# Adaptive-norm transformer block on one core: a reordered prologue, weight tests in pairs on ScalarE, gates computed per feature

## The chip, the cores and the metric

The kernel runs on one core of one Trainium2 chip. The core has five engines with instruction queues of their own: TensorE (PE, with its weight load PEld), VectorE (DVE), ScalarE (ACT), GpSimd (POOL) and SyncE (SP), which only issues DMAs here. They wait for one another through semaphores. The metric is the device time of one execution in microseconds (us).

## The reference, cut to what matters

For four sequences (B = 4) of 2048 tokens with 256 features, one block of attention and one feed-forward network:

```python
mod = (_silu(c) @ wmod).reshape(4, 6, 1, 256)
sa, ca, ga, sb, cb, gb = (mod[:, k] for k in range(6))
ga = (2 * (ga >= 0) - 1) * jnp.maximum(jnp.abs(ga), 0.25)      # gb alike
h = _layernorm(x) * (1 + ca) + sa
x = x + ga * attention(h)        # chunks of 64 tokens, a 64x64 state per head carried from chunk to chunk
h = _layernorm(x) * (1 + cb) + sb
x = x + gb * ffn(h)              # silu(x w1 s) * (x w2 s), two 1024x1024 gelu layers, w3
```

The attention needs, for each chunk and head, the inverse of a unit triangular 64x64 matrix whose entries carry powers of a decay per head. The feed-forward weights are ternary (-1, 0, 1) in the inputs drawn here, but the kernel must be right for others too.

## The kernel before, in words

**Steps.** The 2048 tokens are 32 chunks of 64. A step handles one chunk of all four sequences: 128 partitions hold two sequences' 64 tokens each, twice (NB = 2). Step n computes attention of chunk n, layers l1 and l2 of the feed-forward network of chunk n-1, and layers l3 and w3 (`y`) of chunk n-2. Each engine walks the same list of named items (`mixed`, `walk`), and each engine does its part of an item. So an engine's order is the order of the list, written out by hand, and nothing else moves it. Steps 3 to 30 are a loop of 14 steps that runs twice.

**The path chosen at run time.** A feed-forward weight that is exact in its upper 16 bits can be multiplied in a fast form (`w_hi`, rounded to fp32r). At the start all 22 slots of weights (8 blocks of 128x128 each, 512 KB) are loaded into `w_raw`; the lower 16 bits of each are tested (`check`), each slot is cast to `w_hi` (`round`), and one flag from all tests (`any_low`, `row_low`, `flag_i`) decides by a branch on every engine between two whole programs. All the feed-forward work lies behind that branch.

**The prologue.** Ahead of the branch stand: the modulation (TensorE L1220, L1235, L1239), its gates (`gates()` on VectorE, `gates` on the others), the decay powers (written to DRAM at L734, read back shifted into `hank` at L738, turned by TensorE L1246 and L1247 into the tables of `tables()`), the first norm (`pre("norm", 1)`, L767, L771), the whole of step 0 (the list `alone`: attention of chunk 0 with nothing beside it) and the front part of step 1 (the list `opening`). Behind the branch comes the rest of step 1 (the list `second`), then step 2 and the loop.

**Names that the steps below use.** `fs` is the forward substitution in 8x8 blocks: `fs 0` sets it up, `fs 1` to `fs 3` are six dependent turns of a shuffle, a product and a subtraction (L842, L844, L846). `expand`, `n 1` to `n 3`, `mi`, `upd` build the inverse; `new` and `state` make the new values and the state; `attn_out` multiplies by `wr_sb` and adds the residual (`gah`, `base` on GpSimd, `x1` on VectorE). `norm2` and `ln2` are the second norm, `parts` splits its result (`xh`, `xl`). `square_t` (L666) is ScalarE's copy between `n 2` and `n 3`. `rounded` counts casts; TensorE waits for it before l1 (L1006), before each l2 item and before step 2's transposes (L1091).

In the kernel before, the tests are divided between ScalarE (13 slots, L644) and VectorE (9 slots, L797), one slot at a time, all 22 casts are GpSimd's (L569), and the gates are computed on 4 partitions x 512 features and spread by a matmul with a selector (L1080).

## Time and profile before

| | |
|---|---|
| median of 3 runs | 1912.02 us (1909.98 to 1915.57) |
| the profiled execution, its own time | 1917.14 us |
| its span in the profile | 1915.3 us |
| TensorE busy | 1824.8 us, 95% |
| VectorE, ScalarE, GpSimd busy | 62%, 50%, 33% |
| granted TensorE clock, mean | 0.978 |

The span is what lies between the first and the last record of the profile; the profiled execution's own time is 1.8 us longer. Of the 40 equal slices of the profile's second part (47.9 us each), TensorE is busy 40, 40 and 70% in the first three and 90% or more in all others, and its granted clock is 0.7, 0.5 and 0.8 of full speed in the first three (its two levels are 1.2 and 2.4 GHz) and full in all others. The DMA engines are 80% busy in the first slice and under 10% after it.

### The profile page before, as it was taken

Reading aid. Unit: us, or ns where it says so; the run is one execution under the profiler, and the core shown is the slowest. Engines: PE = TensorE matmul, PEld = TensorE weight load, DVE = VectorE, ACT = ScalarE, POOL = GpSimd, SP = SyncE. Lnnn points to the kernel's source line nnn. Section 1 sums busy time; section 2 is a strip of 40 time slices with the busy share of each in tenths; the row PEclk is TensorE's granted clock in tenths of the full one; section 3 lists DMA queues with packets and bytes.
Section 4 is the critical chain, followed back from the end, with each engine's and each line's share of the span. In section 5 each row is a group of like instructions: output and inputs, shape, how many; then the busy total and the mean of one; then the engine's idle time right before and its main releaser. Section 6 shows DMA issues by size and latency. Waiting matters only on the chain.

```text
span 1915.3 us, 66858 instructions
## 1 busy us (share of the span) xinstructions
PE 1824.8 (95%) x28586; PEld 1746.7 (91%) x28586; DVE 1181.6 (62%) x3051; ACT 965.4 (50%) x2304; POOL 632.1 (33%) x708
## 2 busy tenths in 40 slices
PE   4479999999999999999999999999999999999999
PEld 2369999999999999999999999999999999999998
DVE  4766665666666666666566666566666656666632
ACT  2235454555555555545455545455555545554554
POOL 3434333223323323333332333332333332333211
PEclk7589999999999999999999999999999999999999
DMA  8000000000000000000000000000000000000000
GB/s 301 24 3 19 19 13 19 8 19 19 18 16 17 19 8 19 19 19 13 19 12 16 18 19 13 19 16 11 19 19 19 13 19 8 19 19 19 9 7 12
DMA packets 32721, 43.75 MB, mean 23 GB/s; under 512 B 8156, under 2 KB 24680, under 8 KB 32424
## 3 DMA queue, kind: packets, MB, share of 16 engines
q1 hardware_dynamic: 30736, 37.19, 6.5%
q8 instruction: 228, 3.74, 0.8%
q10 hardware_dynamic: 1688, 2.26, 0.4%
q14 instruction: 69, 0.57, 0.1%
HBM read 22.52 MB, written 8.39 MB: 16 GB/s over the span
## 4 chain that ended last, share of the span: by engine, by line
PE 59%; issue 19%; POOL 10%; DVE 9%; ACT 2%; DMA 1%; SPq 0%; POOLq 0%; DVEq 0%; ACTq 0%
PE mlp L1006 38%; PE mlp L1065 6%; PE solo L1006 4%; PE solo L1105 3%; POOL rinv L537 2%; POOL rg L577 2%; PE solo L1127 2%; POOL gah L550 2%; POOL base L554 2%; DVE h L767 1%; DVE h L771 1%; POOL rstd L537 1%; PE duo L1147 1%; PE duo L1151 1%; DVE kg L815 1%
## 5 line engine op out<-in xcount | busy, mean ns | idle before, releaser
L1006 PE MATMUL mlp<-act_hi,w_hi 128*128 128x256 f32 x4096 | 1007.6, 288 | 2.9 <-DVE full L903 2.1
L1006 PE MATMUL mlp<-act_lo,w_hi 128*128 128x256 f32 x4096 | 972.3, 279 | 0.0
L1006 PEld LDWEIGHTS mlp<-act_hi,w_hi 128*128 128x128 f32 x4096 | 770.4, 188 | 15.0 <-DVE full L903 2.6
L1006 PEld LDWEIGHTS mlp<-act_lo,w_hi 128*128 128x128 f32 x4096 | 771.1, 188 | 1.6
L718 ACT ACTIVATE full<-mlp,scale_sb 128x256 f32<-128x256 f32 x512 | 244.2, 477 | 562.0 <-PE mlp L1006 561.6
L790 DVE TENSOR_TENSOR act_lo<-full,act_hi 128x256 fp32r<-128x256 f32 x512 | 250.0, 488 | 404.0 <-ACT act_hi L719 404.0
L591 POOL TENSOR_TENSOR act_lo<-full,act_hi 128x256 fp32r<-128x256 f32 x256 | 186.5, 735 | 518.4 <-ACT act_hi L708 518.4
L719 ACT ACTIVATE act_hi<-mlp,scale_sb 128x256 fp32r<-128x256 f32 x512 | 240.6, 470 | 0.0
L557 POOL TENSOR_TENSOR lv<-gram,level_mask 128x256 f32<-128x256 f32 x192 | 159.8, 859 | 110.6 <-DVE low L831 104.9
L1006 PE MATMUL mlp<-xh,w_hi 128*128 128x256 f32 x768 | 187.7, 283 | 7.1 <-issue 5.5
L1006 PE MATMUL mlp<-xl,w_hi 128*128 128x256 f32 x768 | 187.0, 282 | 0.0
L537 POOL TENSOR_TENSOR rstd<-ve,minus_half 128x2 f32<-128x2 f32 x64 | 49.3, 770 | 391.5 <-DVE ve L757 391.5
L1006 PEld LDWEIGHTS mlp<-xh,w_hi 128*128 128x128 f32 x768 | 145.7, 190 | 7.7 <-issue 5.9
L903 DVE SCALAR_TENSOR_TENSOR full<-mlp,scale_sb,gate 128x256 f32<-128x256 f32 x192 | 92.7, 483 | 96.1 <-ACT gate L703 96.1
L703 ACT ACTIVATE gate<-mlp,scale_sb 128x256 f32<-128x256 f32 x192 | 91.3, 475 | 117.7 <-PE mlp L1006 117.7
L1006 PEld LDWEIGHTS mlp<-xl,w_hi 128*128 128x128 f32 x768 | 146.1, 190 | 0.0
L1065 PE MATMUL mlp<-w_hi,act_hi 128*128 128x256 f32 x512 | 123.3, 284 | 0.0
L1065 PE MATMUL mlp<-w_hi,act_lo 128*128 128x256 f32 x512 | 122.2, 280 | 0.0
L537 POOL TENSOR_TENSOR rinv<-ssm,minus_half 128x8 f32<-128x8 f32 x32 | 52.6, 1645 | 207.3 <-DVE ssm L780 207.3
L708 ACT CAST act_hi<-full 128x256 fp32r<-128x256 f32 x256 | 101.7, 397 | 12.3 <-DVE full L903 12.3
L1065 PEld LDWEIGHTS mlp<-w_hi,act_hi 128*128 128x128 f32 x512 | 96.5, 188 | 0.4
L1065 PEld LDWEIGHTS mlp<-w_hi,act_lo 128*128 128x128 f32 x512 | 96.6, 189 | 0.0
(157 smaller groups left out, 2642.0 us busy)
## 6 DMA issues: line engine op xcount, KB each, us to landing
w_raw<-in_wts SPq DMA_DIRECT2D x22, 512.0 KB, 13.6
xin<-in_x SPq DMA_DIRECT2D x64, 128.0 KB, 2.8
out_y<-y SPq DMA_DIRECT2D x64, 128.0 KB, 2.5
kg<-r SPq DMA_DIRECT2D x64, 126.0 KB
wmod_sb<-in_wmod ACTq DMA_DIRECT2D x1, 1024.0 KB, 8.6
kg<-last SPq DMA_DIRECT2D x64, 2.0 KB
last<-r SPq DMA_DIRECT2D x64, 2.0 KB, 1.7
wmod_sb<-in_wmod ACTq DMA_DIRECT2D x1, 512.0 KB, 5.3
```

Of the source, the lines that this page charges most:

```text
L537: pool.tensor_tensor(dst[:], src[:], minus_half[:, 0:src.shape[1]], ALU.pow).then_inc(done, 1)
L557: return pool.tensor_tensor(lv[slot][:, e].rearrange("p (b q) n -> p b (q n)", b=NB), gram[:, e].rearrange("p (b q) n -> p b (q n)", b=NB) ...
L591: pool.tensor_tensor(act_lo[0][:, k, :], full[k % 3][:], act_hi[0][:, k, :].bitcast(F32), ALU.subtract).then_inc(l_ready[0], 1)
L703: act.activation(gate[k % 2][:], gated[k % 3][:, 0:TOK], ACT.Silu, scale=scale_sb[:, 0, k:k + 1]).then_inc(l_act[0], 1)
L708: act.copy(act_hi[0][:, j, :], full[j % 3][:]).then_inc(l1_hi, 1)
L718: act.activation(full[k % 2][:], mlp[k % 2][:, 0:TOK], ACT.Gelu, scale=s)
L719: act.activation(act_hi[layer % 2][:, k, :], mlp[k % 2][:, 0:TOK], ACT.Gelu, scale=s).then_inc(l_act[layer], 1)
L790: dve.tensor_tensor(act_lo[layer % 2][:, k, :], full[k % 2][:], act_hi[layer % 2][:, k, :].bitcast(F32), ALU.subtract).then_inc(l_ready[la ...
L903: dve.scalar_tensor_tensor(full[k % 3][:], up, s, gate[k % 2][:], ALU.mult, ALU.mult).then_inc(prod_ready, 1)
L1006: mm = pe.matmul(dst, *general_ops, start=is_first and i == 0, stop=is_last and i == 1)
L1065: mm = pe.matmul(mlp[k][:, 0:D], *ops, start=j == 0 and i == 0, stop=j == HK - 1 and i == 1)
L1105: mm = pe.matmul(solo[0][:, b * D:(b + 1) * D], hT[:, kt, b, :], wv_sb[:, kt, :], start=kt == 0, stop=kt == KT - 1)
```

## The change

Six things are changed, all ahead of step 2; the items of the loop are the same in the same order.

1. The tests are ScalarE's alone, two slots at a time (11 tests of 2048 halves in place of 22 of 1024), and VectorE has none. ScalarE also does 17 of the 22 casts: 4 in step 0, 5 at the end of `opening`, 8 behind the items of l2. GpSimd does the last 5.
2. The gates are computed as columns: TensorE makes them as 128 features x 4 sequences (L1223 of the kernel after), VectorE works on 128x16 and 128x8 elements instead of 4x512, ScalarE spreads them over 64 columns each (`spread`), and TensorE transposes them (8 transposes) into the rows where the selector's product stood. One small input is gone (`sel`).
3. On ScalarE the two copies of the second half of the modulation (`mods`) stand ahead of the wait for the decay powers and the read of `hank`; on SyncE the weight loads from the fifth on wait until `hank` is there.
4. On TensorE the two matmuls with `hank` stand behind the transposes of the first norm (item `tables`) in place of ahead of step 0.
5. `alone` and `opening` are reordered: in `alone`, `fs` is no longer interrupted, the residual (`residual`) and the product with alpha (`wr`) come later; in `opening`, `gram` stands ahead of the second norm on TensorE, and `intra`, `fs 0` and five casts stand ahead of the branch.
6. In `second`, VectorE does `u` and all of `fs 1` to `fs 3` before the first l1 item; `expand`, `far` and `n 1` to `n 3` stand between the l1 items, and `keys` to `attn_out` between the l2 items as in a step of the loop.

```diff
-CHECKS_ACT = {0: (0, 1, 2), 2: (4, 6, 7, 9), 4: (11, 13), 7: (15, 17, 19, 20)}
-CHECKS_DVE = {1: (3, 5), 3: (8,), 4: (10,), 5: (12,), 6: (14, 16), 7: (18, 21)}
+CHECKS = {0: (0,), 1: (1, 2, 3, 4, 5), 2: (6,), 3: (7, 8, 9, 10)}
+ROUNDS_ACT = {0: range(0, 4), 1: range(4, 9)} | {2 + k: (9 + k,) for k in range(8)}
+ROUNDS_POOL = {2 + k: (17 + k,) for k in range(5)}
...
-    alone = [("check", 0), ("ready", 0), ("start", 0), ("tables", 0), ("gram", 0), ("pred", 0), ("values", 0), ("check", 1), ("intra", 0), ("fs", 0), ("far", 0),
-             ("check", 2), ("round", 0), ("fs", 1), ("gates", 0), ("fs", 2), ("fs", 3), ("expand", 0), ("n", 1), ("check", 3), ("round", 1), ("n", 2),
-             ("check", 4), ("n", 3), ("check", 5), ("keys", 0), ("mi", 0), ("check", 6), ("upd", 0), ("round", 2), ("new", 0), ("check", 7), ("state", 0),
-             ("attn_out", 0)]
+    alone = [("check", 0), ("ready", 0), ("start", 0), ("spread", 0), ("tables", 0), ("gram", 0), ("pred", 0), ("values", 0), ("gates", 0), ("intra", 0),
+             ("u", 0), ("fs", 0), ("fs", 1), ("fs", 2), ("fs", 3), ("expand", 0), ("far", 0), ("check", 1), ("round", 0), ("residual", 0), ("n", 1), ("n", 2),
+             ("check", 2), ("wr", 0), ("n", 3), ("keys", 0), ("mi", 0), ("upd", 0), ("new", 0), ("check", 3), ("state", 0), ("attn_out", 0)]
...
-    opening = [("start", 0), ("norm2", 0), ("ln2", 0), ("ln2", 1), ("gram", 0), ("pred", 0), ("values", 0), ("parts", 0), ("silu", 0)]
+    opening = [("start", 0), ("gram", 0), ("norm2", 0), ("ln2", 0), ("ln2", 1), ("pred", 0), ("values", 0), ("intra", 0), ("fs", 0), ("parts", 0),
+               ("round", 1), ("silu", 0)]
+    second = [("u", 0), ("fs", 1), ("fs", 2), ("fs", 3)]
     for item in layers[:len(layers) - len(late)]:
-        second += [item] + ([("round", 3 + item[1])] if item[0] == "l2" else []) + after_layer.get(item, [])
+        second += [item] + {("l1", 0): [("expand", 0), ("far", 0)], ("l1", 1): [], ("l1", 2): [("n", 1)]}.get(item, between.get(item, []))
+        second += [("round", 2 + item[1])] if item[0] == "l2" else []
...
             for u in range(SLOTS):
+                if u == 4:
+                    sp.wait_ge(pow_in, 32)
                 sp.dma_start(w_raw[:, SLOT * u:SLOT * (u + 1), :].rearrange("p b n -> p (b n)"), wts[u]).then_inc(hi_in[u // UNIT_SLOTS], 16)
...
+                        for i in CHECKS[k]:
+                            act.wait_ge(hi_in[i], 16 * UNIT_SLOTS)
+                            after(act, checked, i)
+                            words = w_raw[:, UNIT_SLOTS * SLOT * i:UNIT_SLOTS * SLOT * (i + 1), :].rearrange("p b n -> p (b n)")
+                            act.activation(low_bits[:], low_halves(words), ACT.Copy, accum_out=slot_low[:, i:i + 1]).then_inc(checked, 1)
+                    if name == "round":
+                        for u in ROUNDS_ACT[k]:
+                            slot = slice(SLOT * u, SLOT * (u + 1))
+                            act.wait_ge(checked, u // UNIT_SLOTS + 1)
+                            act.copy(w_hi[:, slot, :], w_raw[:, slot, :]).then_inc(rounded[0], 1)
...
                         if isinstance(n, int) and n == 2:
-                            pe.wait_ge(rounded, SLOTS)
+                            pe.wait_ge(rounded[0], 17)
+                            pe.wait_ge(rounded[1], SLOTS - 17)
```

**ScalarE at the start.** The rows are ScalarE's instructions in their order, each with its line, what it writes and reads, its shape and the semaphores it waits for; `decay_powers` and `hank` are the decay powers' way through DRAM, `low_bits` is a weight test. Before:

```order
L734 DMA decay_powers<-pow_row_sb 4x128 [waits pow_row]
L738 DMA hank<-decay_powers 64x4x64 [waits pow_out]
L738 DMA hank<-decay_powers 64x4x64
L740 COPY mods<-duo 128x256 [waits mod_full]
L741 ACTIVATE mods<-duo 128x256
L644 ACTIVATE low_bits,slot_low<-w_raw 128x1024 [waits hi_in0]
```

ScalarE at the same place in the kernel after:

```order
L717 DMA decay_powers<-pow_row_sb 4x128 [waits pow_row]
L719 COPY mods<-duo 128x256 [waits mod_full]
L720 ACTIVATE mods<-duo 128x256
L724 DMA hank<-decay_powers 64x4x64 [waits pow_out]
L724 DMA hank<-decay_powers 64x4x64
L619 ACTIVATE low_bits,slot_low<-w_raw 128x2048 [waits hi_in0]
```

The two copies have moved ahead of the wait for `pow_out`, and one test of two slots follows where three of one slot each did.

**ScalarE in the middle of step 0**, kernel after; `mods<-mlp` are the gates, `w_hi` is a cast of one slot, `square_t` what `n 3` waits for:

```order
L632 COPY mods<-mlp 128x512 [waits gates_spread] x2
L619 ACTIVATE low_bits,slot_low<-w_raw 128x2048 [waits hi_in1,checked,small_in,cols_ready]
L619 ACTIVATE low_bits,slot_low<-w_raw 128x2048 [waits checked,hi_in2]
L619 ACTIVATE low_bits,slot_low<-w_raw 128x2048 [waits checked,hi_in3]
L619 ACTIVATE low_bits,slot_low<-w_raw 128x2048 [waits checked,hi_in4]
L619 ACTIVATE low_bits,slot_low<-w_raw 128x2048 [waits checked,hi_in5]
L624 CAST w_hi<-w_raw 128x1024 [waits checked] x4
L650 COPY square_t<-duo 128x256 [waits square_full]
```

In the kernel before, four tests of one slot stand ahead of the gates' copies and nothing between these and `square_t`; now five double tests and four casts stand there.

**VectorE behind the branch.** The rows are VectorE's from the first of step 1's second part on; `full` is the product of an l1 item, `sub` and `sub_term` are the substitution. Before:

```order
L903 SCALAR_TENSOR_TENSOR full<-mlp,scale_sb,gate 128x256
L822 TENSOR_TENSOR intra<-duo,intra_mask 128x256 x2
L827 TENSOR_TENSOR v<-v,duo 128x2x4x64
L903 SCALAR_TENSOR_TENSOR full<-mlp,scale_sb,gate 128x256
L831 TENSOR_REDUCE low<-lv 128x64
```

VectorE at the same place in the kernel after (the three rows of `sub_row`, `sub_term` and `sub` stand six times before the row of `full`; the first turn is shown, then the last row of the sixth):

```order
L807 TENSOR_TENSOR v<-v,duo 128x2x4x64
L822 STREAM_SHUFFLE sub_row<-sub 128x64
L824 TENSOR_TENSOR sub_term<-sub_row,low 128x64
L826 TENSOR_TENSOR sub<-sub,sub_term 128x64
...
L826 TENSOR_TENSOR sub<-sub,sub_term 128x64
L883 SCALAR_TENSOR_TENSOR full<-mlp,scale_sb,gate 128x256
L829 TENSOR_TENSOR inv<-sub,con 128x256
```

The first product of l1 stood first on VectorE; now it stands behind nineteen instructions of the attention.

## Rows read from the trace of the kernel before

**Rows 1.** By stretch: us; busy PE, PEld, DVE, ACT, POOL (instructions); clock; DMA share; GB/s.
```profile
45.00:75.00 30.00, 10.17 (x416) 9.30 (x416) 25.99 (x53) 12.21 (x24) 17.40 (x17) 0.50 0.07 20
...
180.00:240.00 60.00, 58.90 (x916) 56.74 (x915) 36.70 (x97) 31.08 (x75) 19.86 (x23) 1.00 0.06 16
```

**Rows 2.** The chain of waits, start: start us, us, what.
```profile
11.93 4.77 DMA decay_powers<-pow_row_sb
...
17.39 9.79 DMA hank<-decay_powers
```

**Rows 3.** Timeline of the first norm: start, length, engine, line, work, [idle before <-releaser].
```profile
18.76 0.88 DVE L767 SCALAR_TENSOR_TENSOR h<-xin,mv,mods 128x256 f32<-128x256 f32 x2 [6.20 <-ACT mods L741]
...
22.29 1.64 POOL L537 TENSOR_TENSOR rinv<-ssm,minus_half 128x8 f32<-128x8 f32 x1 [9.06 <-DVE ssm L780]
...
25.99 0.67 DVE L783 TENSOR_TENSOR r<-h,rinv 128x512 f32<-128x512 f32 x1
```

**Rows 4.** DMA issues: KB each, median us from issue to landing.
```profile
xin<-in_x SPq DMA_DIRECT2D x64, 128.0 KB, 2.8
```

**Rows 5.** Timeline, from the tables to the corrected values.
```profile
34.90 1.18 POOL L577 TENSOR_TENSOR rg<-rT,head_decay 128x512 f32<-128x512 f32 x1 [10.97 <-DVE head_decay L936]
...
42.46 0.69 DVE L827 TENSOR_TENSOR v<-v,duo 128x512 f32<-128x512 f32 x1 [4.54 <-ACT v L656]
```

**Rows 6.** Timeline of the substitution, with GpSimd at work and without.
```profile
45.57 3.99 POOL L569 CAST w_hi<-w_raw 128x1024 fp32r<-128x1024 f32 x4
...
46.72 0.95 DVE L846 TENSOR_TENSOR sub<-sub,sub_term 128x64 f32<-128x64 f32 x1
...
52.71 0.23 DVE L846 TENSOR_TENSOR sub<-sub,sub_term 128x64 f32<-128x64 f32 x1
```

**Rows 7.** ScalarE's tests and casts, all of each line: ns min/median/max.
```profile
L644 ACT ACTIVATE low_bits<-w_raw x13: 1056/1057/1060, 18.6 to 74.3; 128x1024 f32<-128x1024 uint16 x13
...
L708 ACT CAST act_hi<-full x256: 393/396/408, 107.1 to 1877.0; 128x256 fp32r<-128x256 f32 x128
```

**Rows 8.** Timeline, step 0 from the third product of the inverse on.
```profile
62.23 1.07 PE L1151 MATMUL duo<-first_two,square_t 32*32 32x32 f32 x64 [1.46 <-DVE first_two L861]
...
70.07 0.59 ACT L686 COPY vn<-solo 128x512 f32<-128x512 f32 x1 [2.11 <-PE solo L1185]
...
76.09 0.68 DVE L871 TENSOR_TENSOR oT<-o_state,duo 128x512 f32<-128x512 f32 x1
```

**Rows 9.** Timeline, second norm, flag and the first layer's start.
```profile
86.52 2.27 DVE L889 SCALAR_TENSOR_TENSOR xn<-x,mv,rstd 128x256 f32<-128x256 f32 x2
...
97.81 0.14 DVE L988 TENSOR_SCALAR flag_i<-row_low 1x1 int32<-1x1 f32 x1
...
102.94 0.55 PE L1006 MATMUL mlp<-xh,w_hi 128*128 128x256 f32 x1 [5.48 <-issue]
```

**Rows 10.** Two stretches of step 1 behind the branch (columns as in rows 1).
```profile
103.00:106.00 3.00, 3.00 (x14) 3.00 (x15) 0.46 (x2) 0.47 (x1) 0.00 (x0) 0.50 0.02 5
...
124.00:127.00 3.00, 3.00 (x30) 2.78 (x33) 0.32 (x1) 0.04 (x1) 0.00 (x0) 0.51 0.02 5
```

**Rows 11.** Timeline of TensorE, step 2's start, and a full step.
```profile
147.61 0.66 PE L1091 MATMUL duo<-con,h 128*128 128x128 f32 x4 [0.99 <-POOL w_hi L569]
...
176.55 0.28 PE L1006 MATMUL mlp<-xh,w_hi 128*128 128x256 f32 x1
...
204.62 0.60 PE L1091 MATMUL duo<-con,h 128*128 128x128 f32 x4
```

**Rows 12.** Chain of waits, one piece per step; then the idle time before L1156.
```profile
385.86 7.54 PE mlp L1006 x64
...
443.30 7.54 PE mlp L1006 x64
...
499.69 7.54 PE mlp L1006 x64
...
  issue: 6.6, 8
```

160 lines of the change are left out of this document (64 added, 96 removed).

## The prediction

> **What bounds the kernel now.** I read the busy times by stretch first. In a stretch of the loop TensorE is busy 58.9 of 60 us at full clock; between 45 and 75 us it is busy 10.2 of 30 us at half clock while VectorE is busy 26.0 [rows 1]. So the loop is TensorE's, and the change leaves the loop's items as they are; what it can win or lose lies ahead of step 2, whose transposes begin at 147.61 us [rows 11]. That moment is what I forecast; the rest is carried along. Then I read the chain of waits at the start and followed it in the timeline: the decay powers' write and their read into `hank`, the tables, the substitution on VectorE, the products of the inverse, VectorE's late `oT`, the second norm, and 5 us between the flag and the first l1 matmul [rows 2, 3, 5, 6, 8, 9].
>
> **First norm and tables.** `h` begins at 18.76 and had waited 6.20 us for ScalarE's copies, which stood behind the wait for the powers' write (landed at 11.93 + 4.77 = 16.70) [rows 2, 3]. With the copies first, `h` begins some 5.1 us earlier, at 13.6. From `h` to `rinv` it is 22.29 - 18.76 = 3.5 us, `rinv` takes 1.64, so `r` can begin at 18.9 in place of 25.99 [rows 3]; the gates, which filled VectorE until then, are now 128x16 elements and end by about 18.8 (seven operations at most 0.23 us each, the price of a 128x64 one [rows 6], from 17.2 on). `hank`: its read took 9.79 us from 17.39, with the weights streaming in the same DMA engines [rows 2]. Now only four slots are ahead. The bounds are 9.79 (no change) and the 2.8 us of an x load twice its size [rows 4]; I take 2.8, since that load runs on a quiet machine as this one then would: 20.2. The transposes of `r` end at 20.7 (0.9 to 1.1 us of TensorE), so `hank` is no longer last. Before, `rg` began 34.90 - 27.18 = 7.7 us behind the landing [rows 2, 5]; of that, 2.6 were the first norm's transposes and `rT`, which now come ahead. So 20.7 + 5.1 puts `rg` at 25.8: **9.1 us ahead**. The weights from the fifth on start at 20.2; 9.4 MB at the 0.4 MB/us that the engines carried before puts the last at about 45, and ScalarE tests them from 60 on: no cost.
>
> By the Trainium skill, "DMA: Bandwidth & Descriptors", Anatomy of one DMA, a DMA has a fixed part of about 2.0 us and the rest goes by bytes. That speaks for the low bound; this trace's 9.79 us differs, and the measurement decides for a loaded machine. By the page `hank` would be there at 19.4 and the sum would not change.
>
> **Substitution.** Up to `u` nothing else changes: 42.46 - 34.90 = 7.6 us [rows 5], so `u` begins at 33.3 and ends at 34.0; `fs 0` ends at 36.0. Of the six turns, two took 4.5 us beside GpSimd's casts (a 128x64 subtraction 0.95 us beside them, 0.23 alone [rows 6]) and four took 3.4 alone. GpSimd now has no casts there, but `far` and the residual, 3 us of it: I take two slow turns and four quick ones, 7.4 us, to 43.4. The product with alpha (2.7 us, in the middle before) is moved behind. So `first_two` is ready at 48.9 on VectorE.
>
> **ScalarE's queue.** The gates' copies end at 35.7 (the eight transposes are 2.1 us at half clock). Then five double tests and four casts stand ahead of `square_t`. A test of 1024 is 1.06 us [rows 7] with 0.19 to read its sum: a double one 2.3 from the rate, 2.5 at most. A cast of 1024 has no row on ScalarE: bounds are the test's 1.06 (same elements, rows 7) and four times the 256-wide cast, 4 x 0.396 = 1.58 [rows 7]; I take 1.06, because the test is the same size. 35.7 + 5 x 2.3 + 4 x 1.06 + 0.4 = 51.9. So `n 3` begins at 52.0, three us later than VectorE would allow, and 62.23 before [rows 8]: **10.2 ahead**. To `vn` it is 7.84 us of unchanged work [rows 8]: 59.9. The state's products end 2.2 us later, and `oT`, which had stood behind four tests on VectorE until 76.09 [rows 8], begins at 62.8: **13.3 ahead**. ScalarE's last four tests end near 70, when `hT` is wanted only at 79.
>
> **Second norm, flag, branch.** From `oT` to `xn` it was 86.52 - 76.09 = 10.4 us [rows 8, 9]; 2.0 of them `xn` stood behind `r` and `rT` on VectorE, though its own inputs were there, and these now come ahead of it. So `xn` begins at 71.2: **15.3 ahead**. From `xn` to the flag the order on TensorE is the same work; `intra` and `fs 0` on VectorE fit under ScalarE's 2.5 us of `h2`. The flag is at 82.5 in place of 97.81, and the 5.0 us of the branch stay: first l1 matmul at 87.6 in place of 102.94 [rows 9], **15.3 ahead**. ScalarE meanwhile does five casts (5.3 us), to 88; if its own branch then takes as long as TensorE's, its first gate is at 93.
>
> **Behind the branch.** VectorE does `u` and six turns, 0.7 + 6 x 0.85 = 5.8 us, before the first product of l1: 93.5. TensorE has three banks, stops after three l1 items, gets `n 1` at 95.1 and l1's fourth item at 96.1. In step 2 the same item began at 176.55 and the next step's transposes at 204.62 [rows 11]: 28.1 us at full clock, to 124.2. To that come: 1.7 us, as after the branch TensorE first runs 3.4 us at half clock (clock 0.50 at 103 to 106 [rows 10]); 2.2 us, as the transposes wait for ScalarE's 17th cast behind the last gelu (0.2 + 0.85 + 1.06), where 0.99 was waited before [rows 11]; 0.6 for `far` beside l1; 1.0 for some six new hand-overs at 0.15 us. 124.2 + 1.7 + 2.2 + 0.6 + 1.0 = 129.7 against 147.61: **17.9 us ahead**. For the profiled execution that is 1917.14 - 17.9 = 1899.2; it stood 5.1 above the median, so for the runs 1912.02 - 17.9 = 1894.1. I forecast 1894.
>
> **The rivals.** *Hank is no quicker* (its read is 9.79 us by its 256-byte pieces and not by the weights). For: the write before it, only 2 KB, also took 4.77 [rows 2]. Against: an x load of twice the bytes takes 2.8 [rows 4]. Tables 6.5 us later, all behind them too, less what ScalarE's queue absorbs (its tests need weights that then come 7 us later too, so nothing): gain 11.6, 1900. Chance 0.10.
>
> *ScalarE is full.* Casts 1.58 and tests 2.5: `n 3` 1.0 + 2.1 later; in l2 a turn of ScalarE is 0.85 + 1.58 = 2.43 against TensorE's 1.88, eight of them with its other 3.2 us make 22.7 against some 20, and the last cast 0.5: 6.3 us in all, gain 12, 1900. For: the 0.396 row. Against: the test's row. Chance 0.11.
>
> *The stalls go further than I count*: the branch on ScalarE is hidden, the three us at `square_t` and the l1 stop come out shorter: gain 23 to 26, 1887. Chance 0.09.
>
> *The loop shifts.* Between 443.30 and 499.69 a step takes 56.39 us, from 385.86 to 443.30 it takes 57.44; the slow ones hold idle time before L1156 with no releaser, 6.6 us in 8 places [rows 12]. If that hangs on where a step's instructions lie, the shorter prologue may move it: 10 more slow steps take 10 us back (1904), all 20 others take 20 (1914). Chance 0.12: 0.05 for at most 10, 0.07 for more.
>
> *The slower one: the clock stays low.* TensorE fell to 0.51 at 124 to 127, after stops of 2 us behind VectorE [rows 10]. If ScalarE's casts between the gelus stop it briefly in each l2 item, all of step 1 from 96 on runs at half clock: the 28.1 us hold some 27 of matmul, which double: 27 - 18 = 9 us slower, 1921. It decides from about 18 us more at half clock on. Against: once VectorE is not late, TensorE has no stops in such items (58.9 of 60 us busy [rows 1]), and ScalarE's turn with a cast, 0.85 + 1.06 = 1.9, is no longer than TensorE's. The Trainium skill, "TensorE: Matmul & The Clock Gate", What's actually happening, says that throttled is the default and activity releases it; the rows agree (0.50 and 0.51 after stops, 1.00 in the loop [rows 1, 10]), and by it a TensorE that is fed from 96 on is soon at full clock. Chance 0.06. My own sum has 0.52 (1889 to 1899).
>
> **Numbers.** Faster by over 0.3% (under 1906.3; 0.3% is what a measurement here tells from none): 0.52 + 0.10 + 0.11 + 0.09 + 0.05 of the loop case = 0.87. Within: 0.07. Slower: 0.06. The range takes in the further gain and both 1900 cases and the smaller loop shift: 1885 to 1906.
>
> **What would show it.** `h` at 13.6, tables at 25.7, `square_t` waiting on ScalarE's queue and not on TensorE, `n 3` at 52, the flag near 82.5, first l1 near 87.6, VectorE's first product near 93.5, step 2's transposes near 129.7 with a wait for ScalarE's cast, and later steps at 56.4 or 57.4. A `hank` landing past 21, a cast over 1.2 us, or a clock of 0.5 past 100 us would make it wrong.

## The result, and the profile after

The changed kernel takes **1883.53 us** (median of 4 runs, 1882.46 to 1885.55), beside 1913.8 for the kernel before on the same chip; the ratio is 0.985, with a 95% interval of 0.982 to 0.987. Five more runs gave 1883.18 and 0.984 (0.983 to 0.985). The prediction had the direction and was too small: 17.9 us forecast, 30 us measured, and 1883.5 lies below the range's 1885.

The profiled execution went from 1917.14 to 1885.55 us, 31.6 less. The same cut that the prediction made, at the transposes of step 2, divides it:

| us | before | after | gain | forecast |
|---|---|---|---|---|
| span up to step 2's transposes | 147.61 | 125.07 | 22.5 | 17.9 |
| span behind them | 1767.7 | 1758.6 | 9.1 | 0 |

So 4.6 us of what was missed lie ahead of step 2, and 9.1 in and behind the loop, whose instructions the change does not touch. The medians put the miss at 10.6 us (1883.5 against 1894.1); the profiled execution of the kernel before was 3 to 5 us above that kernel's medians.

First the stretches (columns as in [rows 1]), to be read beside [rows 1, 10]:

```profile
45.00:75.00 30.00, 17.69 (x450) 14.94 (x439) 16.61 (x37) 18.51 (x29) 8.93 (x9) 0.56 0.10 26
86.00:89.00 3.00, 2.84 (x13) 2.88 (x14) 1.52 (x8) 1.04 (x3) 0.00 (x0) 0.50 0.02 5
92.00:95.00 3.00, 3.00 (x142) 2.84 (x141) 1.90 (x5) 1.83 (x5) 2.60 (x5) 1.00 0.02 5
98.00:101.00 3.00, 3.00 (x18) 3.00 (x16) 0.97 (x2) 1.53 (x4) 0.92 (x2) 0.55 0.00 0
180.00:240.00 60.00, 59.01 (x919) 56.90 (x918) 38.14 (x103) 30.88 (x74) 19.82 (x23) 1.00 0.06 15
```

VectorE's 26 busy us of [rows 1] are 16.6, TensorE's 10.2 are 17.7. Behind the branch the clock is full already at 92, and then falls once more, to 0.55 at 98 to 101.

The timeline of the kernel after, with the lines that answer to [rows 3, 5, 8, 9, 11] (start, length, engine, line, work, idle time before it):

```profile
14.07 0.88 DVE L750 SCALAR_TENSOR_TENSOR h<-xin,mv,mods 128x256 f32<-128x256 f32 x2 [1.54 <-ACT mods L720]
...
19.33 0.69 DVE L766 TENSOR_TENSOR r<-h,rinv 128x512 f32<-128x512 f32 x1 [0.49 <-POOL rinv L512]
...
20.98 1.06 PE L1069 MATMUL solo<-hank,con 128*128 128x256 f32 x2
...
25.98 1.18 POOL L552 TENSOR_TENSOR rg<-rT,head_decay 128x512 f32<-128x512 f32 x1 [6.75 <-DVE head_decay L916]
...
33.42 0.69 DVE L807 TENSOR_TENSOR v<-v,duo 128x512 f32<-128x512 f32 x1 [6.78 <-ACT v L640]
...
44.54 3.87 ACT L624 CAST w_hi<-w_raw 128x1024 fp32r<-128x1024 f32 x4
...
48.31 0.36 ACT L650 COPY square_t<-duo 128x256 f32<-128x256 f32 x1
...
50.64 1.07 PE L1139 MATMUL duo<-first_two,square_t 32*32 32x32 f32 x64 [0.60 <-DVE first_two L841]
...
61.24 0.69 DVE L851 TENSOR_TENSOR oT<-o_state,duo 128x512 f32<-128x512 f32 x1 [2.74 <-PE duo L1183]
...
69.44 2.89 DVE L869 SCALAR_TENSOR_TENSOR xn<-x,mv,rstd 128x256 f32<-128x256 f32 x2
...
81.58 0.14 DVE L967 TENSOR_SCALAR flag_i<-row_low 1x1 int32<-1x1 f32 x1
...
81.77 0.69 DVE L807 TENSOR_TENSOR v<-v,duo 128x512 f32<-128x512 f32 x1
...
86.16 0.55 PE L985 MATMUL mlp<-xh,w_hi 128*128 128x256 f32 x1 [4.93 <-ACT w_hi L624]
...
88.75 0.48 DVE L883 SCALAR_TENSOR_TENSOR full<-mlp,scale_sb,gate 128x256 f32<-128x256 f32 x1 [1.23 <-ACT gate L687]
...
96.46 0.24 PE L1144 MATMUL duo<-inv,step_nt 32*32 32x32 f32 x2 [1.38 <-issue]
...
125.07 0.66 PE L1079 MATMUL duo<-con,h 128*128 128x128 f32 x4 [1.86 <-ACT w_hi L624]
```

Read it from the top. `h`, `r`, the tables' matmuls (right behind the transposes of `r`, not waiting for `hank`) and `rg` stand where the forecast put them, to half a us. From `square_t` on, everything up to the first l1 matmul is one to three us earlier than forecast. The two lines at 81.58 and 81.77 are the surprise: VectorE goes on 0.05 us behind the flag, and its six turns end at 87.5, under TensorE's 4.9 us of waiting; the first product of l1 comes at 88.75, not at 93.5. The row at 96.46 is a stop of TensorE for which the profile names no releaser, in the middle of 64 equal matmuls.

The tests and casts, all of each line (answering to [rows 7]; ns min/median/max):

```profile
L619 ACT ACTIVATE low_bits<-w_raw x11: 1907/1910/1933, 17.9 to 65.2; 128x2048 f32<-128x2048 uint16 x11
...
L624 ACT CAST w_hi<-w_raw x17: 1027/1044/1082, 44.5 to 124.0; 128x1024 fp32r<-128x1024 f32 x17
```

In the loop one piece of the chain of waits, and the same piece one step later (L985 is L1006 of [rows 12]):

```profile
415.61 7.47 PE mlp L985 x64
...
471.71 7.47 PE mlp L985 x64
```

This step takes 56.10 us; the one shown before took 56.39. From transposes to transposes, steps 2 to 30, the middle step takes 56.23 us and took 56.40, which makes 5 us in 29 steps. The other 4 us are long steps: before, nine were over 56.8 us and all steps together stood 8.4 us above 29 middle ones; after, it is four steps and 4.1 us.

### The profile page after: what moved, and what is told of

It is laid out like the page before. It is cut to its first block, busy times and chain, and to the rows that moved or that the text cites. A ratio compares the mean times of both kernels' runs of the same rounds, so it can differ in the third digit from the quotient of the medians.

```text
span 1883.7 us, 66867 instructions
## 1 busy us (share of the span) xinstructions
PE 1821.0 (97%) x28598; PEld 1747.3 (93%) x28598; DVE 1148.9 (61%) x3042; ACT 987.5 (52%) x2318; POOL 613.2 (33%) x691
## 4 chain that ended last, share of the span: by engine, by line
PE 57%; issue 21%; POOL 11%; DVE 8%; ACT 2%; ACTq 0%; POOLq 0%; DVEq 0%
PE mlp L985 36%; PE mlp L1044 6%; PE solo L985 4%; PE solo L1093 3%; POOL rinv L512 3%; POOL rg L552 2%; POOL gah L525 2%; PE solo L1115 2%; POOL base L529 2%; DVE h L754 1%; DVE h L750 1%; POOL rstd L512 1%; DVE ss L761 1%; PE duo L1139 1%; PE duo L1135 1%
## 5 line engine op out<-in xcount | busy, mean ns | idle before, releaser
L985 PE MATMUL mlp<-act_hi,w_hi 128*128 128x256 f32 x4096 | 1009.2, 289 | 0.4 <-POOL act_lo L566 0.2
L985 PE MATMUL mlp<-act_lo,w_hi 128*128 128x256 f32 x4096 | 974.2, 279 | 0.0
L985 PEld LDWEIGHTS mlp<-act_hi,w_hi 128*128 128x128 f32 x4096 | 769.5, 188 | 12.0 <-POOL act_lo L566 0.4
L985 PEld LDWEIGHTS mlp<-act_lo,w_hi 128*128 128x128 f32 x4096 | 771.7, 188 | 1.6
L773 DVE TENSOR_TENSOR act_lo<-full,act_hi 128x256 fp32r<-128x256 f32 x512 | 244.2, 477 | 410.6 <-ACT act_hi L703 410.6
L985 PE MATMUL mlp<-xh,w_hi 128*128 128x256 f32 x768 | 183.1, 280 | 4.9 <-ACT w_hi L624 4.9
L985 PE MATMUL mlp<-xl,w_hi 128*128 128x256 f32 x768 | 182.6, 280 | 0.2 <-issue 0.2
L985 PEld LDWEIGHTS mlp<-xh,w_hi 128*128 128x128 f32 x768 | 146.4, 191 | 5.3 <-ACT w_hi L624 5.3
L687 ACT ACTIVATE gate<-mlp,scale_sb 128x256 f32<-128x256 f32 x192 | 91.0, 474 | 112.1 <-PE mlp L985 96.1
L985 PEld LDWEIGHTS mlp<-xl,w_hi 128*128 128x128 f32 x768 | 146.5, 191 | 0.4 <-issue 0.4
```

The costliest lines, as they stand in the source:

```text
L687: act.activation(gate[k % 2][:], gated[k % 3][:, 0:TOK], ACT.Silu, scale=scale_sb[:, 0, k:k + 1]).then_inc(l_act[0], 1)
L773: dve.tensor_tensor(act_lo[layer % 2][:, k, :], full[k % 2][:], act_hi[layer % 2][:, k, :].bitcast(F32), ALU.subtract).then_inc(l_ready[la ...
L985: mm = pe.matmul(dst, *general_ops, start=is_first and i == 0, stop=is_last and i == 1)
```

## The experiments

In one table, from the profiled execution of each kernel: when step 2's transposes begin, and what is left of the span behind them; then the median of its runs, and the ratio to the kernel before, run beside it. That kernel's own median lay between 1912.1 and 1913.8 from one set of runs to the next, so differences of one or two us between rows are not told from none. Three of the kernels (dve_branch, no_branch, second_old) ran on another chip than the rest. Nor do the profiled executions start alike: `h` begins between 13.1 and 15.0 us in the kernels whose order up to there is that of the kernel after.

| kernel | step 2 at | the rest | median | ratio to before |
|---|---|---|---|---|
| before | 147.61 | 1767.7 | 1913 | 1 |
| after | 125.07 | 1758.6 | 1883.5 | 0.985 (0.982, 0.987) |
| after_again | 124.98 | 1757.4 | 1883.2 | 0.984 (0.983, 0.985) |
| after_pad32 | 126.52 | 1766.1 | 1892.7 | 0.988 (0.985, 0.990) |
| before_shift32 | 146.26 | 1756.8 | 1904.0 | 0.995 (0.994, 0.996) |
| after_align64 | 123.40 | 1766.5 | 1892.9 | 0.989 (0.988, 0.991) |
| act64 | 123.35 | 1748.2 | 1875.1 | 0.981 (0.979, 0.982) |
| dve_branch | 126.22 | 1755.4 | 1881.5 | 0.983 (0.981, 0.985) |
| no_branch | 122.82 | 1757.1 | 1881.8 | 0.984 (0.982, 0.986) |
| second_old | 129.06 | 1760.1 | 1892.1 | 0.990 (0.987, 0.992) |
| no_hold | 133.64 | 1755.1 | 1889.6 | 0.988 (0.986, 0.989) |
| mods_late | 129.66 | 1759.3 | 1889.9 | 0.987 (0.984, 0.989) |
| single_tests | 121.77 | 1757.6 | 1882.4 | 0.984 (0.982, 0.986) |
| pass28 | 122.40 | 1752.6 | 1877.2 | 0.982 (0.980, 0.983) |
| ishift128 | 122.40 | 1755.6 | 1879.9 | 0.982 (0.981, 0.984) |
| best | 122.19 | 1742.9 | 1865.5 | 0.975 (0.973, 0.977) |

### The nine us in the loop: addresses

The change makes `slot_low` 11 numbers long in place of 22. That takes 64 bytes of each partition in place of 96, so all that is allocated later, `xh` and `xl` among it, lies 32 bytes lower.

**after_pad32** (after, with the old addresses)
```diff
     slot_low = sb("slot_low", [SLOTS // UNIT_SLOTS])
+    pad = sb("pad", [8])
```


> The kernel after with an unused tensor of 8 floats behind slot_low, so that every tensor allocated later stands at the address it has in the kernel before (xh and xl 32 bytes past a multiple of 64 in place of on one). Theory A (the address of xh and xl sets the spacing of the l1 matmuls): a normal step goes from 56.17 back to 56.39 us, about 29 times 0.2, so 1889 to 1890 us, with nothing changed ahead of step 2. Rival (the shorter prologue or the queues' order did it, addresses do nothing): 1883 to 1885 us, steps 56.17.

**before_shift32** (before, with the new addresses)
```diff
-    slot_low = sb("slot_low", [SLOTS])
+    pad = sb("pad", [SLOTS // 2])
...
+        slot_low = sb("slot_low", [SLOTS], F32, early)
```


> The kernel before, with slot_low moved into the region that is used again later and an unused tensor of 11 floats in its place, so that all later tensors stand at the addresses of the kernel after, 32 bytes lower. Theory A (address): a normal step 56.39 to 56.17 us, 5 to 6 us off the total, 0.997 of before (1906 to 1908 us), step 2 still begins near 147.6. Rival (address does nothing): ratio 1.000.

**after_again** is the control.


> The kernel after, unchanged, as the control of this call and for a second trace. Both theories: 1883 to 1885 us. If the long steps of the loop (about 1 us longer, idle TensorE ahead of the bursts of 32x32 matmuls) belong to places in the program, they are the same steps as in the first trace (steps 4 and 18 to 20 of the marks); if they are chance, they are others.

Both point to the address, and more strongly than expected. 32 bytes up cost the kernel after 9.5 us, 32 bytes down give the kernel before 9.4. Their "rest" columns simply trade places: 1766.1 and 1756.8 against 1757.4 to 1758.6 and 1767.7. One run of after_pad32 fell out: of its five, four took 1891.6 to 1894.5 us and one 1882.6; it has no trace, and I can't explain it. The groups of l1's matmuls in the loop (205 to 1760 us) show where; the number behind the busy time is the mean ns of one. First before and before_shift32:

```profile
L1006 PE MATMUL mlp<-xh,w_hi 128*128 128x256 f32 x649 | 157.2, 281 | 0.0
```
```profile
L1007 PE MATMUL mlp<-xh,w_hi 128*128 128x256 f32 x672 | 157.3, 277 | 0.0
```

and then after and after_pad32:

```profile
L985 PE MATMUL mlp<-xh,w_hi 128*128 128x256 f32 x672 | 157.5, 277 | 0.0
```
```profile
L986 PE MATMUL mlp<-xh,w_hi 128*128 128x256 f32 x672 | 162.8, 281 | 0.0
```

The 4 ns go with the address, not with the kernel: 64 such matmuls a step make 0.26 us. TensorE's time in the middle one of steps 3 to 29, divided by what it works on (from the start of one matmul to that of the next, us), shows that this is not the only part that goes with the address:

| | l1 | l2 and l3 | w3 | attention |
|---|---|---|---|---|
| before | 8.05 | 31.50 | 3.81 | 13.09 |
| before_shift32 | 7.80 | 31.61 | 3.83 | 12.88 |
| after | 7.80 | 31.63 | 3.83 | 12.88 |
| after_pad32 | 8.05 | 31.56 | 3.81 | 13.05 |

L1 gains 0.25 us from the lower addresses, attention 0.2, and l2 and l3 lose 0.1. Which operand does it in the attention was not tried. The middle step follows: 56.40 and 56.45 at the old addresses, 56.19 to 56.23 at the new ones, 6 or 7 us in 29 steps. Of before_shift32's larger gain behind step 2 (10.9 us in the profiled executions) the rest is again fewer long steps, four against nine. The control's long steps were others than those of the first trace: one over 56.8 us (59.0, step 16), where the first has four (steps 3, 18, 19 and 30). So their number is not a property of the program alone, and whether the address has a hand in it is not shown.

**after_align64** asks whether 64 bytes are the unit.
```diff
+            if -(-int(np.prod(shape)) // 8) % 2:
+                c.enter_context(nc.sbuf_tensor(name + "_pad", [P, 8], F32))
```


> The kernel after with every tensor in SBUF begun on a multiple of 64 bytes (act_hi and act_lo, which in the kernel after are 32 past one, as well as xh and xl). Theory A in its wide form (any moving operand off a multiple of 64 costs): l2 and l3, four times as many matmuls as l1, gain too, up to 0.5 us a step, 1870 to 1878 us. In its narrow form (only some reads are slower when off): 1883 to 1885, since the kernel before with act_hi on a multiple of 64 had no quicker l2. Rival (address does nothing): 1883 to 1885.

They are not: it lost 9.7 us to after_again, and its `xh` matmul takes 283 ns. So I measured the spacing by itself.

**addresses**
```diff
+            for step32 in range(64):
+                off = 8 * step32
+                for w in range(4):
+                    for j in range(KT):
+                        for part in range(2):
+                            at = off + 512 * part + 256 * j
+                            mm = pe.matmul(mlp[w % 2][:, 0:TOK], w_hi[:, KT * w + j, :], data[:, at:at + 256],
+                                           start=j == 0 and part == 0, stop=j == 1 and part == 1)
```


> The kernel after, with 1024 more matmuls of l1's form behind its last output, on TensorE alone: 16 (four weight pairs, two halves each, two operands 2048 bytes apart) at each of 64 start addresses of the moving operand, 32 bytes apart, over 2048 bytes, all at full clock. Nothing else runs then. Theory A1 (TensorE's own reads cost more at some addresses): the spacing of the starts changes with the address, from about 113 to 117 ns, with a period that the row shows. Rival A2 (the address only matters because other engines read or write SBUF at the same time): all 64 are spaced alike, within 1 ns.

Nine of the 64 groups, 16 matmuls each, in TensorE's timeline. They begin 160, 192, 224, 0, 32, 64, 96, 128 and 160 bytes past a multiple of 256:

```profile
1925.57 2.05 PE L1242 MATMUL mlp<-act_hi,w_hi 128*128 128x256 f32 x16
...
1927.46 2.05 PE L1242 MATMUL mlp<-act_hi,w_hi 128*128 128x256 f32 x16
...
1929.35 2.07 PE L1242 MATMUL mlp<-act_hi,w_hi 128*128 128x256 f32 x16
...
1931.25 2.07 PE L1242 MATMUL mlp<-act_hi,w_hi 128*128 128x256 f32 x16
...
1933.15 2.04 PE L1242 MATMUL mlp<-act_hi,w_hi 128*128 128x256 f32 x16
...
1935.03 1.99 PE L1242 MATMUL mlp<-act_hi,w_hi 128*128 128x256 f32 x16
...
1936.86 2.05 PE L1242 MATMUL mlp<-act_hi,w_hi 128*128 128x256 f32 x16
...
1938.75 2.08 PE L1242 MATMUL mlp<-act_hi,w_hi 128*128 128x256 f32 x16
...
1940.66 2.05 PE L1242 MATMUL mlp<-act_hi,w_hi 128*128 128x256 f32 x16
```

From start to start over 16, that is 118.1, 118.1, 118.8, 118.8, 117.5, **114.4**, 118.1, 119.4 ns, and then it repeats. A1 holds, A2 falls: no other engine runs here. Counted like this, with the weights at 128 past, the sizes of the tensors put `xh` and `xl` of the kernel after at 64 past (114.4), of the kernel before at 96 (118.1), of after_align64 at 128 (119.4): the order of 277, 281 and 283. By the sweep, l1 gains 64 x 3.7 ns = 0.24 us a step.

**pairs** moves the weights as well.
```diff
+                                at, wat = 8 * m32 + 512 * part + 256 * j, 8 * w32 + 128 * (KT * w + j)
+                                mm = pe.matmul(mlp[w % 2][:, 0:TOK], weights[:, wat:wat + 128], data[:, at:at + 256],
```


> The kernel after, with 1024 more matmuls of l1's form behind its last output: 8 start addresses of the weights, 32 bytes apart, times 8 of the moving operand, 32 bytes apart, 16 matmuls for each pair. The earlier sweep, with the weights at 128 past a multiple of 256 bytes, gave spacings of 114.7 to 119.6 ns that repeat every 256 bytes of the moving operand's address. Theory D1 (the two reads collide: what counts is the distance between the two addresses modulo 256): each row of eight is the row before shifted by one, and its best is where the moving operand stands 64 below the weights. Rival D2 (the moving operand's own address counts): all eight rows alike, best at 64 past a multiple of 256, 114.7 ns. D3 (chance of the layout): no order.

Weights at 64 past, moving operand at 0 and at 64 past; then weights at 128 past, moving operand at 64 past:

```profile
1961.52 2.00 PE L1242 MATMUL mlp<-act_hi 128*128 128x256 f32 x16
...
1965.12 2.08 PE L1242 MATMUL mlp<-act_hi 128*128 128x256 f32 x16
...
1995.48 1.99 PE L1242 MATMUL mlp<-act_hi 128*128 128x256 f32 x16
```

The same operand at 64 past is among the slowest with weights at 64 and the quickest with weights at 128, where 16 matmuls take 0.09 us less. All 64 spacings, worked out from the records (ns, first start to last of a group, over 15):

```
weights   moving operand at, past a multiple of 256 bytes
at        160   192   224     0    32    64    96   128
160     125.8 118.2 117.9 119.2 119.1 117.3 114.5 117.8
192     118.3 119.5 118.1 117.8 119.3 119.1 117.3 114.5
224     117.8 118.2 119.5 118.2 117.8 119.2 119.1 117.3
  0     117.6 115.5 117.8 119.6 118.1 117.9 119.3 119.1
 32     118.7 117.3 114.7 117.8 119.6 118.1 117.9 119.2
 64     119.6 118.3 117.3 114.7 117.9 119.5 118.2 117.8
 96     117.9 119.9 118.6 118.7 113.6 117.9 119.5 118.1
128     116.7 117.8 119.2 119.1 117.3 114.5 117.8 119.6
```

Apart from a few places, the first above all (125.8), each row is the row above shifted by one. In seven of the eight the best (113.6 to 115.5 ns) stands 64 below the weights; the one exception, weights at 224 with 117.8, I can't explain. D1 holds: the distance modulo 256 counts.

**act64** uses it where it pays most, in l2 and l3.
```diff
+    pad_act = sb("pad_act", [40])
     act_hi = [sb(f"act_hi{i}", [HK, TOK], F32R) for i in range(2)]
...
+    pad_xh = sb("pad_xh", [24])
     xh = sb("xh", [KT, TOK], F32R)
```


> The kernel after with act_hi, act_lo, xh and xl all begun 64 bytes past a multiple of 256 (in the kernel after xh and xl are, act_hi and act_lo are 160 past one), by two unused tensors of 160 and 96 bytes. Theory A1 from the sweep: 118.2 ns becomes 114.7 for the 256 matmuls of l2 and l3 in a step, 0.9 us a step, and 31 steps: 28 us faster than after, 1855, as far as no other engine takes over. Rival (the sweep's numbers do not carry over to the full kernel, where l2's spacing is set by weight loads or other engines): 1883 to 1885. In between, if VectorE or ScalarE set part of a step: 1860 to 1875.

8.1 us faster than after: the direction right, the size a third of the forecast's 28. Most matmuls of l2 and l3 are then 113 to 114 ns apart, but about a third stay at 117 to 119, and before act64 they were on average 117, not the 118.2 of the sweep. L2 and l3 take 31.1 us of a middle step in place of 31.6, where the forecast wanted 0.9 us less, and attention 0.15 more than in the kernel after; the middle step takes 55.9 us in place of 56.2. What keeps the third back was not tried.

### The stop at 95 us, and where instructions lie

**pass28** and **ishift128** ask about TensorE's idle times that nothing releases.
```diff
-PASS = 14
+PASS = 28
```


> The kernel after with the loop's 28 steps in one pass in place of two passes of 14, so that TensorE never jumps back. Theory E (the long steps, 56.9 to 58.7 us near steps 17 to 21, are TensorE's wait for instructions behind the jump back): they vanish, 2 to 3 us faster, 1880 to 1881. Rival (they come from where the instructions lie, or from chance): as many long steps, elsewhere, 1883 +- 1.


```diff
             with pe.If(any_bits > 0):
                 program(True)
+                for _ in range(128):
+                    pe.wait_ge(const_in, 16)
```


> The kernel after with 128 more waits at the end of TensorE's slow path, which is never run; the fast path's instructions then lie that much further on and are otherwise the same. Theory F (TensorE's stalls in the bursts of 32x32 matmuls are waits for instructions, and where the instructions lie decides whether a burst meets one): the stall of 1.4 us at 95 us vanishes or changes by over 0.3 us, long steps are others, total 1879 to 1886. Rival (stalls belong to the work itself, or to the time since the branch): the same 1.4 us at the same matmul, 1883 +- 1.

Neither changes an instruction that is run ahead of the loop, and in both the stop at 95 us is gone. The stretch 95 to 98 us of after (98 to 101 stands above), and both of ishift128:

```profile
95.00:98.00 3.00, 1.62 (x18) 1.50 (x11) 0.42 (x1) 0.00 (x0) 0.46 (x1) 0.88 0.02 5
```
```profile
95.00:98.00 3.00, 2.99 (x76) 2.84 (x63) 1.19 (x3) 1.36 (x5) 1.02 (x2) 1.00 0.02 5
98.00:101.00 3.00, 3.00 (x84) 2.79 (x82) 2.27 (x6) 2.38 (x6) 2.62 (x4) 1.00 0.01 3
```

A stop of 1.38 us costs 2.7: the clock falls to 0.55 behind it, and step 2 comes at 125.07 in place of 122.40. Theory F has its prediction for the stop: unused instructions on a path that is not run take it away, and the total is 3.3 us less. The other traces bear it out: the stop stands, 1.37 to 1.71 us long, in all seven traces of kernels that keep TensorE's instructions where the kernel after has them and change neither a test nor a branch (both of the kernel after, after_pad32, after_align64, act64, no_hold, mods_late), and in none of the three in which they lie further on (pass28, ishift128, best). The stop of 1.5 us near 50 us, whose instructions stand ahead of the branch and were not moved, is still there in all three (1.0 to 2.1 us). That the stop is a wait for instructions is not shown by this; that it hangs on where they lie is. For the long steps F is not shown: from step 2 on pass28 has one over 56.8 us, ishift128 two, after four, and after_again one. Theory E (the jump back) is at most half of it: ishift128, which still jumps back, has 3.3 of pass28's 6 us, and pass28's one long step (step 17) is where the second pass used to begin. A point against F in its simple form is single_tests below, where TensorE's program is the same as in the kernel after and the stop is 0.3 us; so another engine's program or timing matters too, and that stays open.

### Behind the branch

**dve_branch** puts to the test the assumption of the prediction.
```diff
+            dve.wait_ge(flag_set, 1)
+            any_bits = dve.value_load(flag_i[0:1, 0:1], min_val=0, max_val=1)
+            with dve.If(any_bits > 0):
+                run(dve, step)
+            with dve.Else():
+                run(dve, step)
```


> The kernel after, with VectorE given the same choice of path that TensorE and SyncE have: it reads the flag and branches between two copies of the same program. In the kernel, VectorE, ScalarE and GpSimd have no branch at all. Theory B (the prediction's step failed because VectorE does not branch; with one it would stall as TensorE does): u begins about 5 us after the flag (87) in place of 0.05 us, the first l1 product comes at 93 to 94, as the prediction had it, and the total is 3 to 5 us longer, 1887 to 1889. Rival (only TensorE is slow behind a branch, by the length of its program or its loads): u begins under 1 us after the flag and the total is within 1 us of 1883.

VectorE's timeline, flag and what follows, then its first product:

```profile
82.92 0.14 DVE L967 TENSOR_SCALAR flag_i<-row_low 1x1 int32<-1x1 f32 x1
86.96 0.69 DVE L807 TENSOR_TENSOR v<-v,duo 128x512 f32<-128x512 f32 x1 [3.89 <-issue]
...
92.63 0.48 DVE L883 SCALAR_TENSOR_TENSOR full<-mlp,scale_sb,gate 128x256 f32<-128x256 f32 x1
```

Half right. With a branch VectorE does stall, 3.9 us, and its first product is 3.9 later than after's 88.75, about where the prediction had it. But the total did not move. This execution began 1 us later than after's (`rT` of step 0 at 22.18 against 21.23), and step 2 came 1.15 later, so only 0.2 us are lost. TensorE now waits 1.36 us for VectorE at 94.1, its stop without a releaser is 1.11 us at 99.2, and at 98 to 101 us its clock is 1.00 where after's is 0.55. What VectorE loses, the clock gives back. That holds beside a kernel that has the stop and its slow clock: from the first l1 matmul to step 2 dve_branch takes 38.5 us, the kernel after 38.9, but ishift128, without the stop, 35.6. What VectorE's branch would cost there was not tried.

**no_branch** (TensorE always takes the fast path; the choice of path is left out)
```diff
-            any_bits = pe.value_load(flag_i[0:1, 0:1], min_val=0, max_val=1)
-            with pe.If(any_bits > 0):
-                program(True)
-            with pe.Else():
-                program(False)
+            program(False)
```


> The kernel after without TensorE's reading of the flag and its branch: it runs the fast program always, right behind the transpose for the flag; SyncE still branches. The choice of path is left out. Theory C (the 4.9 us between the flag and the first l1 matmul are hidden to two thirds, since VectorE works on u and fs until 87.5 and the first product cannot come sooner than about 88): the first l1 matmul comes at 81 to 83, waiting for ScalarE's first cast, TensorE does three l1 items and stops; gain 1 us or less. Rival (the branch is on the path): 4 to 5 us faster, 1878 to 1879.

The first l1 matmul comes at 82.82, step 2 at 122.82, 2.2 us sooner, and the median is 1.4 to 1.7 lower, which is no more than the sets of runs differ by. Theory C's side. But this edit moves TensorE's instructions too, and the stop at 95 us is gone, which alone is worth 2.7 us. The fair comparison is ishift128, which has the branch and not the stop: from the flag to step 2 it takes 40.7 us, no_branch 40.2 and the kernel after 43.5. So the branch itself is worth about 0.5 us. TensorE has its three items done early and then waits 4.0 us for VectorE's `inv_t`: nearly all of the branch is hidden behind VectorE's work.

**second_old** (the old order of step 1 behind the branch)
```diff
-    second = [("u", 0), ("fs", 1), ("fs", 2), ("fs", 3)]
+    after_layer = {("l1", 0): [("u", 0)], ("l1", 3): [("fs", 1), ("far", 0)], ("l1", 5): [("fs", 2)], ("l1", 7): [("fs", 3), ("expand", 0)],
+                   ("l2", 0): [("n", 1)], ("l2", 1): [("n", 2)], ("l2", 2): [("n", 3)], ("l2", 3): [("keys", 0), ("mi", 0)], ...}
```


> The kernel after with the old order of step 1 behind the branch: l1's first item, then u, two turns of fs at a time behind l1's items 3, 5 and 7, and the inverse's products between the l2 items. Prediction's view: the six turns under the branch are worth what VectorE no longer does beside l1 and l2, so step 2's transposes begin 3 to 6 us later (128 to 131) and the total is 1886 to 1889. Rival (the order behind the branch is worth nothing, since VectorE has room there): within 1 us of 1883. Third (a small loss turns into many stops of TensorE with the clock at half, as before): 6 to 10 us, 1890 to 1893.

8.6 us slower by the medians, which is the third case; the profiled executions are 5.5 us apart, and step 2 at 129.06 (4.0 later) lies where the prediction's view had it. Three stretches of it show TensorE stopped behind VectorE (1.05, 2.10 and 2.99 us) and then on the low clock, from 98.9 to 109.2:

```profile
98.00:101.00 3.00, 2.38 (x16) 2.08 (x14) 2.74 (x7) 2.27 (x5) 2.91 (x4) 0.65 0.00 0
101.00:104.00 3.00, 0.63 (x48) 0.66 (x52) 2.46 (x4) 1.19 (x2) 1.47 (x2) 0.50 0.01 3
104.00:107.00 3.00, 3.00 (x47) 2.94 (x36) 0.87 (x2) 0.00 (x0) 0.00 (x0) 0.50 0.03 5
```

### Ahead of the branch

**no_hold**
```diff
-                if u == 4:
-                    sp.wait_ge(pow_in, 32)
```


> The kernel after without SyncE's wait for hank ahead of the fifth weight load: all 22 loads are queued at once, as before. Prediction's view: hank's read takes 9.8 us beside them in place of 3, so it lands near 23 to 27, and with the tables all that follows comes 3 to 6.5 us later, 1887 to 1890. Rival (hank's read is as long without the weights, or its landing is hidden by the first norm): within 1 us of 1883.

6.1 us slower (8.6 at step 2). Its chain of waits has the read of `hank` at about its old length, 10.31 us, and TensorE waits for it:

```profile
17.59 10.31 DMA hank<-decay_powers
```
```profile
27.95 1.22 PE L1067 MATMUL solo<-hank,con 128*128 128x256 f32 x2 [6.16 <-DMA hank<-decay_powers]
```

So the wait on SyncE's queue is worth some 6 us. In the kernel after, the read had landed at 19.85, 2.65 us from its issue, so the prediction's rival *Hank is no quicker* is refuted; its price, 6.5 at the tables, was right (`rg` at 33.10 for 25.98, in an execution that began 0.6 later).

**mods_late**
```diff
             act.wait_ge(pow_out, 16)
             for c in range(2):
                 act.dma_start(hank[half(c)], shifted).then_inc(pow_in, 16)
+            act.wait_ge(mod_full, 2)
+            act.copy(sa[:, 1, :], duo[1][:, 1, 0:D])
```


> The kernel after with ScalarE's two copies of the modulation again behind the wait for the decay powers and the issue of hank's read. Prediction's view: h starts 5.1 us later (18.8 to 19.2), r near 24, rT near 26, and since hank is there at 20.9 the tables wait for TensorE behind r's transposes: everything is 4 to 5 us later, 1887 to 1888. Rival (the first norm is not what the tables wait for): 1884 or less.

`h` begins at 18.18, the matmuls with `rg` at 31.43 against 27.30, step 2 at 129.66: 4.6 us later, as expected; the runs' median is 6.4 over after's, more than that, and spread (1883.2 to 1891.7). The stop behind the branch is 1.70 us here, 1.38 in the kernel after.

**single_tests**
```diff
+                            for u in (2 * i, 2 * i + 1):
+                                after(act, checked, u)
+                                words = w_raw[:, SLOT * u:SLOT * (u + 1), :].rearrange("p b n -> p (b n)")
+                                act.activation(low_bits[:, 0:SLOT * P], low_halves(words), ACT.Copy, accum_out=slot_low[:, u:u + 1]).then_inc(checked, 1)
```


> The kernel after with 22 tests of 1024 halves in place of 11 of 2048, all on ScalarE; all addresses that the loop uses are kept. A test of 1024 took 1.06 us and 0.19 to read its sum, two of them about 2.5, against 2.10 for a double one: the ten ahead of square_t cost 2 us more, so n 3, which waited for ScalarE at 48.3, starts up to 2 us later, less what VectorE's queue takes (first_two at 50.07, n 3 at 50.64): 0.5 to 1.5 us, 1884 to 1885. Rival (pairing matters more, 3 us and up, since ScalarE's whole queue to the flag is late): 1886 and over.

A miss. The median is 1882.4, no slower at all. `square_t` comes at 48.93 (48.31 in after), but TensorE had a stop of 1.5 to 1.8 us of the kind above in both just then, which ended with the same eleven matmuls, so the later copy is covered. The stop at 95 us is 0.3 here, which by itself brings step 2 forward; but step 2 at 121.77 is no later than in the kernels without that stop either (122.2 to 122.4). In both kernels, in TensorE's timeline, single_tests first:

```profile
48.66 0.42 PE L1146 MATMUL duo<-inv,step_nt 32*32 32x32 f32 x11 [1.80 <-issue]
```
```profile
49.62 0.42 PE L1144 MATMUL duo<-inv,step_nt 32*32 32x32 f32 x11 [1.52 <-issue]
```

The pairing of tests is worth nothing that these runs can measure.

### The version that beats both

**best** is act64 and pass28 together.
```diff
-PASS = 14
+PASS = 28
...
+    pad_act = sb("pad_act", [40])
...
+    pad_xh = sb("pad_xh", [24])
```


> The kernel after with both of the earlier gains: act_hi, act_lo, xh and xl at 64 past a multiple of 256 bytes (64 below the weights, modulo 256), and the loop in one pass of 28 steps. If the two are independent: 8 + 6 = 14 us off, 1869. If the shorter matmuls only give the stalls for instructions more room (the bursts come sooner behind one another): 1871 to 1874. If pass28's gain was the place of its instructions and not the missing jump, and that place stays the same here: 1869 too, with no stall at 95 us.

1865.5 us, 18 less than after and 2.5% less than before; more than the sum of the two, 14. Its steps take 55.86 us almost without exception, only three in a row, 16 to 18, take 56.5, 57.2 and 56.6, and there is no stop at 95 us.

## Why the prediction was too small

**First norm and tables: right.** Forecast for `h`, `r`, `hank` and `rg` 13.6, 18.9, 20.2 and 25.8; measured 14.07, 19.33, 19.85 and 25.98. The time of 19.4 that the prediction works out for `hank` from the Trainium skill is close too, though the section that it cites describes DMAs issued by GpSimd, and this one is ScalarE's. no_hold and mods_late show both halves by their absence: 6.1 us and 4.6 to 6.4.

**Substitution: right.** `u` 33.3 forecast, 33.42 measured; the six turns were to end at 43.4 and ended at 43.0.

**ScalarE's queue: the place right, the sizes high.** The gates' copies ended at 34.3 where I took 35.7, a double test is 1.91 + 0.19 = 2.10 where I took 2.3, a cast 0.97 apart where I took 1.06. `square_t` came at 48.31 in place of 51.5: 1.5 us of that are the start of the queue, 1.2 the tests and 0.5 the casts. `n 3` came at 50.64 and not 52.0, and the queue was no longer what it waited for: TensorE's own stop of 1.52 us held `first_two`. This is 1.4 us of the 4.6, and it is carried to the flag (81.58 for 82.5) and to the first l1 matmul (86.16 for 87.6).

**The branch: the assumption was false.** I wrote that VectorE's `u` and six turns begin at the first l1 matmul and that ScalarE's "own branch takes as long as TensorE's"; the section on the kernel says that every engine branches. The code says otherwise: only TensorE and SyncE have an `If`; VectorE, ScalarE and GpSimd run one program. So the first product came at 88.75 in place of 93.5 to 94.1, and l1's fourth item at 91.75 in place of 96.1. That is 4.4 us, 1.4 of them carried along from ScalarE's queue, and they stood to step 2. dve_branch shows that this reading is too simple as a cause: with VectorE late by 3.9 us the end is the same, because the clock then stays up. From l1's fourth item to step 2 I had 33.6 us and it took 33.3, which is luck: about 3 of these are a stop that I did not foresee, and its slow clock. Without it (ishift128) the same stretch takes 30.2. So of the 5.5 us that I added to step 2's 28.1 (1.7, 2.2, 0.6 and 1.0), only 2.1 are real in a TensorE that is fed, and 1.86 of those are the wait for the cast. The 1.7 for the half clock was booked in the wrong place: the clock rose at 90.4, ahead of the fourth item.

**The rival that came nearest.** *The stalls go further than I count* had a gain of 23 to 26 at a chance of 0.09; the gain ahead of step 2 is 22.5. ScalarE has no branch that could stall it, and the waits at `square_t` and at l1 came out shorter, as it says. Its total was short of the loop's part all the same.

**"The rest is carried along": the step that failed.** The prediction cut the time at step 2 and held that the loop's items are unchanged and so is their time. 9.1 of the 13.7 us that the profiled execution was below the forecast come from there. The items are unchanged; their operands' addresses are not. My rival *The loop shifts* named the shorter prologue and the place of instructions, and only as a loss. The diff had the line that did it: `slot_low` with half its numbers. That the 32 bytes are worth 9.4 to 9.5 us is shown from both sides, by after_pad32 and before_shift32. That l1's matmuls are a part of it, 0.25 us a step, is shown in isolation by the sweep; the attention's 0.2 us and the number of long steps are not explained. With the addresses held, in after_pad32, the change is worth 20.7 us, 2.8 more than the forecast's 17.9: without the addresses, the forecast would have been nearly right in size, in part because its errors ahead of step 2 and the stop at 95 us work against each other.

**The slower rival**, a clock that stays low, did not come: 1.00 from 101 us on. But second_old shows that it was near: with the old order behind the branch the clock is low for 10.3 us between 98.9 and 109.2, and the kernel is 5.5 (profiled) to 8.6 us (medians) slower.
